# An attention block with a routed feed-forward layer: the opening, the search for the second batch's tokens and the end put in another order

## What is computed

```
attn = softmax(Q1 K1^T / sqrt(128)) - lam * softmax(Q2 K2^T / sqrt(128))
O    = attn V ; O = O / rms(O) * rms_scale * (1 - LAMBDA_INIT) ; y = O Wo
x    = layernorm(X + y)
```

```
probs = softmax(x gate_w) ; top_p, top_idx = top_k(probs^T, 256)
out[top_idx] += (gelu(x[top_idx] w1) w2) * top_p
x     = layernorm(x + out)
```

## Time and profile before

| | us |
|---|---|
| median of 3 runs (930.83 to 931.35) | 931.21 |
| the profiled execution | 930.3 |
| its span | 928.6 |

### The profile page before, as it was taken

One profiled execution on the slowest core, in us unless ns is written; L12 is line 12 of the kernel. 1 busy time (PEld: TensorE's weight loads), 2 busy tenths in 40 slices (PEclk: granted clock), 3 DMA queues, 4 the chain that ended last, 5 costly groups with the idle time before them and its releaser, 6 DMA issues.

```text
span 928.6 us, 15029 instructions
## 1 busy us (share of the span) xinstructions
PE 873.8 (94%) x4654; PEld 736.2 (79%) x4656; DVE 708.2 (76%) x1209; ACT 748.7 (81%) x1454; POOL 643.3 (69%) x1031
## 2 busy tenths in 40 slices
PE   6899999999999999999999999999999999876964
PEld 4678888888888888888888888888888887766953
DVE  5777777777777777777777768789998886597755
ACT  4888888888888888888888888888888897766642
POOL 3766767676776767676778766777676778696851
PEclk9999999999999999999999999999999999879997
DMA  5010001000000000000101110101000011331241
GB/s 165 1 29 1 29 1 29 1 27 4 7 23 1 29 1 29 0 30 1 30 1 42 34 30 3 29 3 30 1 17 2 9 32 42 102 85 30 46 72 46
DMA packets 42271, 25.44 MB, mean 27 GB/s; under 512 B 5408, under 2 KB 40256, under 8 KB 42192
## 3 DMA queue, kind: packets, MB, share of 16 engines
q1 hardware_dynamic: 38864, 21.20, 7.9%
q0 software_dynamic: 3328, 3.28, 2.2%
HBM read 20.14 MB, written 4.33 MB: 26 GB/s over the span
## 4 chain that ended last, share of the span: by engine, by line
PE 81%; DVE 6%; POOL 4%; issue 3%; ACT 3%; DMA 1%; another core or an unknown queue 0%; SPq 0%; POOLq 0%; DVEq 0%; ACTq 0%
PE t_ps L1483 11%; PE ring_a L1446 6%; PE ring_a L1448 6%; PE ring_a L1447 6%; PE ring_b L1446 6%; PE ring_b L1448 6%; PE ring_b L1447 6%; PE u_ps L1446 6%; PE u_ps L1448 6%; PE u_ps L1447 6%; PE o_ps L1446 3%; PE o_ps L1447 2%; PE o_ps L1448 2%; PE x_ps L1446 1%; PE x_ps L1448 1%
## 5 line engine op out<-in xcount | busy, mean ns | idle before, releaser
L587 POOL TENSOR_TENSOR attn<-prob 128x1024 f32<-128x1024 f32 x128 | 306.9, 2398 | 177.8 <-ACT prob L741 169.3
L982 DVE TENSOR_TENSOR at_lo<-t_ps,at_hi 128x512 fp32r<-128x512 f32 x253 | 173.9, 687 | 91.7 <-ACT at_hi L724 91.4
L975 DVE TENSOR_REDUCE negmax<-ring_a 128x1 f32<-128x1024 f32 x128 | 156.7, 1224 | 62.6 <-PE ring_a L1448 60.6
L724 ACT ACTIVATE at_hi<-t_ps 128x512 fp32r<-128x512 f32 x253 | 151.7, 600 | 40.1 <-PE t_ps L1483 39.3
L975 DVE TENSOR_REDUCE negmax<-ring_b 128x1 f32<-128x1024 f32 x128 | 156.0, 1219 | 1.7 <-PE ring_b L1448 0.9
L1483 PE MATMUL t_ps<-ident,attn 128*128 128x128 f32 x1012 | 152.1, 272 | 3.7 <-DVE at_lo L982 3.5
L741 ACT ACTIVATE prob<-prob,coef 128x1024 f32<-128x1024 f32 x128 | 147.6, 1153 | 2.6 <-POOL coef L549 2.6
L1483 PEld LDWEIGHTS t_ps<-ident,attn 128*128 128x128 f32 x1012 | 124.9, 140 | 28.9 <-DVE at_lo L982 8.3
L735 ACT ACTIVATE prob<-ring_a,negmax 128x1024 f32<-128x1024 f32 x128 | 142.9, 1116 | 5.8 <-DVE negmax L975 5.2
L735 ACT ACTIVATE prob<-ring_b,negmax 128x1024 f32<-128x1024 f32 x128 | 142.6, 1114 | 1.2 <-DVE negmax L975 1.2
L1446 PE MATMUL ring_b<-xt_hi,q_hi 128*128 128x512 f32 x256 | 111.5, 435 | 2.3 <-ACT prob L735 2.3
(11 more groups left out here) (440 smaller groups left out, 1834.8 us busy)
## 6 DMA issues: line engine op xcount, KB each, us to landing
attn<-in_L_ffn_w SPq DMA_DIRECT2D x12, 256.0 KB, 3.3
wq_s<-in_L_attn_Wq SPq DMA_DIRECT2D x16, 128.0 KB, 2.5
wk_s<-in_L_attn_Wk SPq DMA_DIRECT2D x16, 128.0 KB, 2.6
wv_s<-in_L_attn_Wv SPq DMA_DIRECT2D x16, 128.0 KB, 2.1
wvt_s<-in_L_attn_Wv_T SPq DMA_DIRECT2D x16, 128.0 KB, 2.5
wot_s<-in_L_attn_Wo_T SPq DMA_DIRECT2D x16, 128.0 KB, 2.7
xres<-in_L_attn_X SPq DMA_DIRECT2D x2, 512.0 KB, 7.7
xg_dram<-xres SPq DMA_DIRECT2D x2, 512.0 KB, 3.7
```

Source lines behind the costliest of these rows:

```text
L587: pool.tensor_tensor(attn[:, t % AB, :], prob[:, t % 2, 1, :], prob[:, t % 2, 0, :], ALU.add).then_inc(attn_ready, 1)
L724: act.activation(at_hi[:, g % 2, half * GT:(half + 1) * GT, c], t_bank(t, half)[:, :].rearrange("p (k q) -> p k q", q=P), ACT.Copy).then_i ...
L975: dve.tensor_reduce(negmax[:, par, m:m + 1], ring[m][:, :], axis=AX.X, op=ALU.max, negate=True).then_inc(negmax_ready, 1)
L982: dve.tensor_tensor(at_lo[:, g % 2, k, c], t_bank(t, half)[:, :].rearrange("p (k q) -> p k q", q=P), at_hi[:, g % 2, k, c].bitcast(F32), A ...
```

## The change

- **Opening**: of the first head's four query pieces two (c = 1) go behind the scores of tile 0 on PE, into tiles 1 and 2 on ACT and DVE. The rounding `xk_hi` of batch b goes behind `row_max(b, 1)`; on POOL `xk_lo` of batch 0 goes to tile 0, that of batch 1 to tile 1, between factor(0) and combine(0). Batch 1's transposed tokens are loaded later, to `xg0`, and split in tiles 20, 28 (ACT) and 24, 32 (DVE); combine(3) no longer waits for that.
- **Before the search**: the gate's second half goes ahead of rows_in(0) on PE; `ln_vars(1, 0)` ahead of a copy on DVE; `gate_rep(1)` on ACT is made in two halves; POOL's weight splits wait for `ln_done` 4, the end of `ln_end(1)`.
- **Search**: one FFN half in each level.
- **POOL**: all eight scatters stand behind the 16 gathers.
- **End**: `add_parts` goes behind half 33 of the FFN, `ln_end(2)` behind `add_mixed`, and batch 1's rows are stored in four parts. ACT's squares for it follow its whole FFN.

```diff
     RAWS = 4
-    LAST = [1, 2, 3, 5, 6, 8, 9, 11]
+    LAST = [lv + 1 for lv in range(LEVELS)]
     assert LEVELS * LB == 32 and REP == 16 and E * TB == NC and CT == 2 and FT == 4 and NCH == 2
...
     M_NORM, M_REP, M_SCAN, M_CHOOSE, M_PICK, M_SPREAD, M_IDX = 91, 92, 118, 120, 122, 123, (125, 126)
+    G_XTHI, G_XTLO = (20, 28), (24, 32)
     WINDOW = [G_GATE, *G_VOTES, G_LIM, G_OFF, G_TOK]
...
-        xt_raw = [prob[:, 0, 0, :], attn[:, 3, :]]
         xg0 = sb("xg0", [P, E * CT * XW])
+        xt_raw = [prob[:, 0, 0, :], xg0[:, 0:N]]
         sq = [xg0[:, 0:N], flat[:, N:2 * N], xk_part(xk_hi, 1), xk_part(xk_lo, 1)]
...
                 sp.dma_start(xt_raw[0][:, c * NC:(c + 1) * NC], XT[0][:, c * NC:(c + 1) * NC]).then_inc(xt_in[c], 16)
-            sp.dma_start(xt_raw[1], XT[1]).then_inc(xt_in[2], 16)
             for b in range(B):
...
             load_qk(1)
+            sp.dma_start(xt_raw[1], XT[1]).then_inc(xt_in[2], 16)
             sp.dma_start(gate_s[:, :], gate_w).then_inc(gate_in, 16)
...
             for b in range(B):
-                for h in range(2):
-                    s = slice(h * GT, (h + 1) * GT)
+                parts = 2 * (b + 1)
+                for h in range(parts):
+                    s = slice(h * QT // parts, (h + 1) * QT // parts)
                     sp.wait_ge(ln_done, 2 * (B + b) + h + 1)
...
                                  x1[:, b * QT:(b + 1) * QT, :][:, s, :]).then_inc(out_done, 16)
-            sp.wait_ge(out_done, 32 * B)
+            sp.wait_ge(out_done, 16 * (2 + 4))
...
-            for b in range(B):
+            def xk_lower(b):
+
                 pool.wait_ge(xk_hi_done, b + 1)
...
                 pool.wait_ge(scaled_ready, t + 1)
-                if t == 3:
-                    pool.wait_ge(xt_split, 4)
                 pool.tensor_tensor(attn[:, t % AB, :], prob[:, t % 2, 1, :], prob[:, t % 2, 0, :],
...
             for G in range(TILES):
+                if G == 0:
+                    xk_lower(0)
                 if exists(G - LAG_C):
                     factor(G - LAG_C)
+                if G == 1:
+                    xk_lower(1)
                 if exists(G - LAG_O):
...
             gather_rows(4, 1)
-            pool.wait_ge(gate_step, 11)
+            pool.wait_ge(ln_done, 4)
             for e in range(2, E):
...
             pool.iota(tok_row, pattern=[[1, N]], base=0, channel_multiplier=0).then_inc(row_ready, 1)
-            for q in range(2):
-                scatter(q)
             gather_ready(1)
...
                     gather_rows(q, k)
-            for q in range(2, E):
+            for q in range(E):
                 scatter(q)
...
                 act.wait_ge(gate_step, 6 * b + 5)
-                act.activation(pr_rep[b].rearrange("p (t e j) -> p t e j", e=E, j=REP),
-                               pr[:, b].unsqueeze(3).broadcast_to([P, QT, E, REP]), ACT.Copy).then_inc(gate_step, 1)
+                for h in range(2):
+                    act.activation(pr_rep[b][:, h * NC:(h + 1) * NC].rearrange("p (t e j) -> p t e j", e=E, j=REP),
+                                   pr[:, b, h * GT:(h + 1) * GT].unsqueeze(3).broadcast_to([P, GT, E, REP]),
+                                   ACT.Copy).then_inc(gate_step, 1)
...
-            for c in range(NCH):
-                for m in range(2):
-                    q_round(0, m, c, (x_ps, t_ps, u_ps, o_ps)[2 * c + m][:, :])
+            for m in range(2):
+                q_round(0, m, 0, (x_ps, t_ps)[m][:, :])
...
                 k, s = (G - 1) // QT, (G - 1) % QT
-                if G == 1:
-                    for c in range(NCH):
-                        act.wait_ge(xt_in[2], 16)
-                        act.activation(xt_hi[:, N + c * NC:N + (c + 1) * NC], xt_raw[1][:, c * NC:(c + 1) * NC],
-                                       ACT.Copy).then_inc(xt_hi_done, 1)
+                if G in G_XTHI:
+                    c = G_XTHI.index(G)
+                    act.wait_ge(xt_in[2], 16)
+                    act.activation(xt_hi[:, N + c * NC:N + (c + 1) * NC], xt_raw[1][:, c * NC:(c + 1) * NC],
+                                   ACT.Copy).then_inc(xt_hi_done, 1)
                 if exists(G - LAG_T1 - 1):
...
                     exponential(G - LAG_E, 1)
+                if G in (1, 2):
+                    q_round(0, G - 1, 1, (u_ps, o_ps)[G - 1][:, :])
                 if s in X_Q and k + 1 < STEPS and G > 0:
...
                 ffn(n)
-                if n == 2 * JOBS:
-                    for c in range(QT):
-                        ln_squares(2, c)
+            for c in range(QT):
+                ln_squares(2, c)
             act.wait_ge(mixed, 1)
...
                                                ALU.add, ALU.mult)
-                last_x.then_inc(ln_done, 1)
+                    if c % GT == GT - 1 or (n == 3 and c % 2 == 1):
+                        last_x.then_inc(ln_done, 1)
...
                 xt_lower(n)
-            for c in range(NCH):
-                for m in range(2):
-                    q_part(0, m, c, (x_ps, t_ps, u_ps, o_ps)[2 * c + m][:, :])
+            for m in range(2):
+                q_part(0, m, 0, (x_ps, t_ps)[m][:, :])
             dve.wait_ge(lam_ps, 1)
...
                               ALU.mult).then_inc(rms_ready, 1)
-            for b in range(B):
+
+            def xk_round(b):
+
                 dve.wait_ge(x_in[b], 16)
...
                 row_max(G, 0)
+                if G in (1, 2):
+                    q_part(0, G - 1, 1, (u_ps, o_ps)[G - 1][:, :])
                 if s in X_Q and k + 1 < STEPS and G > 0:
...
                     wp_parts(k)
-                if G == 1:
-                    for n in range(NCH, 2 * NCH):
-                        xt_lower(n)
+                if G in G_XTLO:
+                    xt_lower(NCH + G_XTLO.index(G))
                 if G % QT == AT_WOT:
...
                 row_max(G, 1)
+                if G < B:
+                    xk_round(G)
                 if G in WINDOW:
...
             ln_means(1, 1)
+            ln_vars(1, 0)
             x1t_copy(1)
-            ln_vars(1, 0)
             ln_vars(1, 1)
...
                     one_hots((n - 2 * E) // 2)
-                if n in (2 * JOBS - 3, 2 * JOBS - 1):
-                    h = (n - 2 * JOBS + 3) // 2
-                    add_parts(h)
-                    ln_means(2, h)
             ffn(2 * JOBS + 1)
+            for h in range(2):
+                add_parts(h)
+                ln_means(2, h)
+            ffn(2 * JOBS + 3)
             ln_vars(2, 0)
             ln_vars(2, 1)
-            for h in range(2):
-                ln_end(2, h)
-            ffn(2 * JOBS + 3)
             dve.wait_ge(mixed, 2)
...
                 ln_means(3, h)
+            for h in range(2):
+                ln_end(2, h)
             ln_vars(3, 0)
...
-                if h == 0:
-                    pe.wait_ge(gate_step, 6 * (b + 1))
+                pe.wait_ge(gate_step, 6 + 6 * b + b * h)
                 for j in range(GT):
...
             pe.wait_ge(m_split, 1)
-            for c in range(NCH):
-                pe.wait_ge(xt_split, c + 1)
-                for m in range(2):
-                    q_product(0, m, c, (x_ps, t_ps, u_ps, o_ps)[2 * c + m][:, :])
+            pe.wait_ge(xt_split, 1)
+            for m in range(2):
+                q_product(0, m, 0, (x_ps, t_ps)[m][:, :])
+            pe.wait_ge(xt_split, NCH)
             pe.wait_ge(lam_diag, 1)
...
                 scores(G, 1, 1)
+                if G == 0:
+                    for m in range(2):
+                        q_product(0, m, 1, (u_ps, o_ps)[m][:, :])
                 r = G - LAG_U
                 if exists(r):
-                    if r == 0:
-                        pe.wait_ge(xk_split, B)
+                    if r % BT == 0:
+                        pe.wait_ge(xk_split, r // BT + 1)
                     if r % GT == 0:
...
             gate(1, range(GT))
+            gate(1, range(GT, QT))
             rows_in(0)
-            gate(1, range(GT, QT))
             ffn(0)
```

## The result

The changed kernel takes 927.98 us (median of 8 runs, 927.04 to 928.35), the kernel before beside it 930.97 (8 runs, 929.46 to 931.35): ratio 0.9969, 95% interval 0.9958 to 0.998. The forecast was 926.6. The profiled execution took 928.21 us with a span of 926.5, against 930.3 and 928.6 before, so of the two traces 2.10 us are to be explained, where the sum had 4.55. The gain is 0.3%; the two ranges of times do not overlap.

The account below looks back on a forecast made before the run. PE was taken to bound the loop, POOL's scatters the tail. Terms 1.5 - 2.1 - 3.9 - 0.1 + 7.6 - 10.05 + 2.5 = -4.55 us take 930.3 to 925.75; with 0.9 for the median, 926.6, own range 924 to 929, outer 922.8 to 931.0.

Parts of the forecast that it names:

- Opening, +1.5: Start of the kernel: combine(0) queued behind batch 1's `xk_lo` on POOL, at 25.6 against 24.10, +1.5 us.
- Loop, 0: Tiles 20 to 32: the moved ACT copies and DVE subtractions cost nothing, as PE does not idle there; 0 us.
- The rival of 2.4 us: Loop: the moved splits stall PE, +2.4 us, 929.0 in all; chance 0.08.
- Loop to search, -2.1: Between loop and search: `ln_end(1)` without POOL's subtractions beside it saves 3.8 us on DVE, of which 2.1 arrive.
- Search, -3.9: Search on DVE: eight levels with one FFN half each take 21.9 us instead of 25.84.
- the rival of 930.1: Search: PE gets too little work and its clock falls to 1.2 GHz, levels and index part longer; chance 0.10.
- Ties to first gather, taken as unchanged: From search to POOL's first gather: no term in the sum; POOL's weight splits end at 843.5, before the indices at 846.
- POOL's queue, +7.6: POOL behind the indices: 16 scatters instead of 12 after the 16 gathers, four more at 1.92 us each, +7.6 us.
- the rival of stretching scatters: POOL's queue: all 16 scatters take 2.46 us each, +8.7 us, 935.3 in all; chance 0.08.
- Read back, taken as 5.2: Tail: from the last scatter's end at 898.3 to the read back at 903.5, 5.2 us.
- DVE's order, -10.05: Tail: only job 15's operand stands behind `add_parts`, so the last mix follows 3.75 us after it instead of 13.8.
- PE waits ten us: Tail: PE is done at 896.6, with the FFN 6 us ahead, and idles ten us before the last mix at 907.2.

Follow-up runs that it names:

- all three unedited traces: The changed kernel with no edit: the first execution, 927.98 us, and two repeats on other chips, 927.26 and 927.03 us.
- the repeats: Two further runs of the changed kernel with no edit, on other chips: 927.26 us (ratio 0.9967) and 927.03 us (ratio 0.9974).
- the third: Second repeat of the changed kernel with no edit, on a chip where the kernel before took 929.91: 927.03 us, ratio 0.9974.
- the old wait: Changed kernel, but POOL starts the weights' remainders behind the gate's last step, as before, not behind `ln_end(1)`: 938.64 us, ratio 1.0047 (disturbed).
- the old shares: Changed kernel, but FFN halves shared over the search levels as before (1, 1, 1, 2, 1, 2, 1, 2): 935.71 us, ratio 1.0015 (disturbed).
- scatter(0) ahead: Changed kernel with scatter(0) ahead of the second batch's gathers: 938.84 us, ratio 1.0053 (disturbed).
- all eight kernels: The first eight edited versions of the changed kernel, run on two other chips: 934.5 to 939.3 us, ratios 1.0010 to 1.0062.

## Why the prediction was right, and where not

The forecast of faster, by the mechanism given, held, and 927.98 lies in the range; of the 4.6 us forecast, 3.0 came in the medians and 2.1 between the two traces. Some terms agree better than their reasons: three of the agreements below are partly luck, and are called so. By its own steps:

- *Opening, +1.5*: mechanism right. combine(0) was held by the second `xk_lo`, +0.79 instead of +1.5: PE's clock rose earlier (scores of tile 0 complete for the maximum at 13.57, forecast 13.95), so the second `xk_lo` started at 22.54 instead of 23.0, and it held POOL for 2.35 us instead of 2.54. But the delay was followed for combine(0) only. After it tile 2 lost 0.44 in this trace, where DVE's maximum of tile 3 was late and PE's clock had fallen, and tile 5 lost 0.37 in all three unedited traces. The prediction had no wait of PE and no fall of its clock behind combine(0). That opening and loop together gave +1.83 for +1.5 is luck: half of the term came from steps that it did not have.
- *Loop, 0*: the step that failed in kind. Steps of 0.47 stood at tiles 24 and 32 in all three unedited traces. The cover named was PE's full occupation and the tiles' lack of a query piece; but those tiles have `u_low` on DVE, and the split stood ahead of a row maximum. The rival of 2.4 us was too dear; what it cost was 0.5 to 1.0.
- *Loop to search, -2.1*: -2.16, `gate_max` +0.90 for +0.8 forecast, and the mechanism confirmed by undoing it. The size is partly luck: the repeats have -2.44 and -3.38, with `gate_max` at +0.56 and +0.08. In the third PE made the gate's sixteen matmuls in 2.99 us instead of 3.42 and had the upper level for part of the row transposes (granted clock 0.70 from 812 to 816, 0.50 in the other two). The prediction's sum has no clock in these steps.
- *Search, -3.9*: 21.97 for 21.9. The clock did fall in the index part (0.74 from 840 to 850), but DVE set the pace of the search, and no level took longer than forecast; the rival of 930.1 did not come about.
- *Ties to first gather, taken as unchanged*: +1.60, the largest miss of the trace, and there in the repeats (+1.13, +2.14). The prediction had POOL's splits end at 843.5 (they ended at 841.39) and asked only whether their results were in time, not what they run beside. 0.49 and 0.83 are the scan and the comparison behind POOL; that it is POOL was shown by two kernels in which the subtractions were over before the scan and the iota before the comparison, and both took their old time: one with the old wait and one with the old shares. The remaining 0.3 goes with them (7.78 us with the old wait, 7.77 in the kernel before); where it sits was not resolved.
- *POOL's queue, +7.6*: +6.69. The gathers took 21.16 us instead of 21.61 and the four scatters 7.1. At 1.89 each in the mean of sixteen, the rival of stretching scatters fell.
- *Read back, taken as 5.2*: 8.09 from the last scatter's start to `add_parts` instead of 6.79. In the unedited repeats it was 7.43 and 7.26, so the first execution's extra is partly chance. SP issues the first read 3.49, 3.37 and 3.58 us behind that start, 3.21 in the kernel before.
- *DVE's order, -10.05*: -10.08, and this too is luck. What sets the last mix is the second half's read: its additions start 9.64, 9.44 and 9.56 us behind the last scatter's start in the three traces, where the forecast had 8.3. The first half's late landing only shifts time from one piece of the ledger to the other; the two together are -8.78, -8.99 and -8.87, not -10.05.
- *PE waits ten us*: it waited 7.89 (7.64 and 9.65 in the repeats). PE was ready at 903.33 (902.99 and 900.52), not at 896.6. Of the 6 us by which the FFN was to run ahead, none to two came, and the wait for the second read covered that. Where they went was not traced.
- *After the last mix, +2.5*: +2.59, the clock at 0.50 in the last mix as forecast.

The view that the end is POOL's was right and incomplete: of the +7.6, 3.7 were avoidable in an idle of 4.68 us that the prediction's own sum left there, as the queue with scatter(0) ahead shows; what that alone is worth in time was not measured.

## What to carry to other kernels

When work is moved off a contended spot, look up what it will run beside next, for every instruction of the other engine that shares its port, and not only whether its result is in time. A queue that has become the bound wants its idle stretches filled first: two scatters fitted where it waited for indices. And in a pipelined loop one spare instruction has its place behind the last row maximum of a tile, not ahead of one, even where the bound engine shows no idle.

## What the runs showed of the hardware that was not expected

- VectorE's scan (`TENSOR_TENSOR_SCAN`, 128x64, both operands in SBUF) is held by GpSimd's two-operand subtraction: 0.78, 1.15 and 0.92 us instead of 0.29. An iota beside the same scan does not hold it (0.29, in the kernel with the old shares). A 256-element comparison took 1.18 us beside an iota of 1.01 (1.06 where the iota had started first), but 0.35 beside a scatter's issue.
- On two chips PE, ScalarE and VectorE stood still together, with 13 to 16 us less of PE's work done by 885 us, during and behind GpSimd's sixteen gathers, in all eight kernels profiled there, while DMA moved as much as elsewhere in the one compared. Reads of instructions (two queues called instruction) are late in these traces: in the first five kernels (up to that with scatter(0) ahead) none is recorded between 852 and 875 us, where the unedited kernel elsewhere has two at 861 and 865. In the other three one stands at 862 to 865 and the next at 874 to 884. That engines ran out of instructions fits this, but an engine that stands for another reason would ask for none either; the cause is open.
- The granted clock fell near the end of the loop, and not in every execution: in four of fourteen traces it is 0.76 from 780 to 787 us, and the last tile comes 1.0 to 1.5 us later there. PE had been busy 8.3 to 9.8 of the ten us before, in the kernel before 8.5 and in the changed one 9.8. In the opening it falls near 28 to 34 us (0.72 or 0.73) in eight of the nine traces in which PE had waited for the late combine(0), and in none of the five others.
